# Splitting an expert's weights in quarter matrices on VectorE, between its tiles of h, instead of on GpSimd

## The reference, cut to what matters

```python
def _L0_ffn_ref(x, gate_weight, w1, b1, w2, b2):
    E, H = (8, 1024)
    logits = jnp.einsum('bld,ed->ble', x, gate_weight)
    kth_val = jnp.sort(logits.reshape(-1))[expert_k - 1]
    mask = (logits >= kth_val).astype(x.dtype)
    gates = logits * mask
    h = jax.nn.gelu(jnp.einsum('bld,ehd->bleh', x, w1) + b1, approximate=True)
    y = jnp.einsum('bleh,edh->blde', h, w2) + b2.T[None, None]
    return jnp.einsum('blde,ble->bld', y, gates)
x = x + jnp.tanh(g_xattn[0]) * _L0_xattn_ref(_layernorm(x), ctx_768, ...)
x = x + jnp.tanh(g_ffn[0]) * _L0_ffn_ref(_layernorm(x), ...)
```

## Time and profile before

| | |
|---|---|
| median of 3 runs | 2202.37 us (2200.15 to 2203.65) |
| the profiled execution: its time | 2204.5 us |
| its span | 2202.7 us |
| TensorE busy in the span | 2003.1 us (91%) |
| VectorE busy | 1359.9 us (62%) |
| ScalarE busy | 719.7 us (33%) |
| GpSimd busy | 230.9 us (10%) |
| granted clock of TensorE, mean | 0.958 |

### The profile page before, as it was taken

One profiled execution on the slowest core, in us unless ns is written; L12 is line 12 of the kernel. 1 busy time (PEld: TensorE's weight loads), 2 busy tenths in 40 slices (PEclk: granted clock), 3 DMA queues, 4 the chain that ended last, 5 costly groups with the idle time before them and its releaser, 6 DMA issues.

```text
span 2202.7 us, 29673 instructions
## 1 busy us (share of the span) xinstructions
PE 2003.1 (91%) x9252; PEld 1446.8 (66%) x9252; DVE 1359.9 (62%) x2389; ACT 719.7 (33%) x1206; POOL 230.9 (10%) x227
## 2 busy tenths in 40 slices
PE   3758999999975999899999989999998998999998
PEld 3643333333334788788778878877887886888887
DVE  7748888888836675645555465465456456454554
ACT  2224766666751222222222222222221222222222
POOL 5210111001114000200110020020002002000000
PEclk9877999999986999999999999999999999999999
DMA  3753322222201000100100010010001001000010
GB/s 108 242 190 111 81 77 73 71 79 78 62 30 60 0 28 18 48 10 15 38 20 14 10 48 14 10 48 14 10 13 49 10 10 47 14 10 15 29 43 34
DMA packets 80059, 103.39 MB, mean 47 GB/s; under 512 B 25986, under 2 KB 44164, under 8 KB 80004
## 3 DMA queue, kind: packets, MB, share of 16 engines
q1 hardware_dynamic: 80004, 102.71, 15.6%
HBM read 76.34 MB, written 26.08 MB: 46 GB/s over the span
## 4 chain that ended last, share of the span: by engine, by line
PE 63%; DVE 6%; ACT 0%; issue 0%; DVEq 0%; ACTq 0%
PE ps_y L1840 31%; PE ps_h L1826 31%; DVE h_lo L2047 3%; DVE h_hi L2043 2%; DVE candidate L2086 0%; ACT gelu L1946 0%; DVE w_hi L1986 0%; DVE gated L2112 0%; DVE out_T_acc L2117 0%; DVE w_lo L1988 0%; PE ps_h L1876 0%; DVE gate L2076 0%; DVE gate L2058 0%; PE ps_h L1908 0%; DVEq L1995 0%
## 5 line engine op out<-in xcount | busy, mean ns | idle before, releaser
L1946 ACT ACTIVATE gelu<-ps_h,b 128x512 f32<-128x512 f32 x512 | 352.0, 688 | 1153.6 <-PE ps_h L1826 1047.2
L2043 DVE CAST h_hi<-gelu 128x512 fp32r<-128x512 f32 x512 | 254.3, 497 | 601.5 <-ACT gelu L1946 601.2
L1840 PE MATMUL ps_y<-h_hi,w_hi 128*128 128x512 f32 x1024 | 410.3, 401 | 42.6 <-DVE h_lo L2047 42.6
L1826 PE MATMUL ps_h<-x_hi,w_hi 128*128 (+1 forms) x1024 | 413.5, 404 | 9.2 <-DVE w_lo L1988 9.2
L2047 DVE TENSOR_TENSOR h_lo<-gelu,h_hi 128x512 fp32r<-128x512 f32 x512 | 408.0, 797 | 16.5
L1826 PE MATMUL ps_h<-x_lo,w_hi 128*128 (+1 forms) x1024 | 411.0, 401 | 0.0
L1826 PE MATMUL ps_h<-x_hi,w_lo 128*128 (+1 forms) x1024 | 410.3, 401 | 0.0
L1840 PE MATMUL ps_y<-h_hi,w_lo 128*128 128x512 f32 x1024 | 408.0, 398 | 0.0
L1840 PE MATMUL ps_y<-h_lo,w_hi 128*128 128x512 f32 x1024 | 407.8, 398 | 0.0
L898 DVE TENSOR_REDUCE low<-ps_s 128x1 f32<-128x512 f32 x512 | 322.0, 683 | 39.8 <-PE ps_s L755 37.8
L1840 PEld LDWEIGHTS ps_y<-h_hi,w_hi 128*128 128x128 f32 x1024 | 195.3, 191 | 96.2 <-DVE h_lo L2047 48.3
(11 more groups left out here) (209 smaller groups left out, 1406.7 us busy)
## 6 DMA issues: line engine op xcount, KB each, us to landing
gate<-gates_scratch SPq DMA_DIRECT2D x64, 256.0 KB, 3.3
q_st<-q_scratch SPq DMA_DIRECT2D x64, 132.0 KB
k_scratch<-k_hl SPq DMA_DIRECT2D x32, 256.0 KB
q_scratch<-q_hl SPq DMA_DIRECT2D x32, 256.0 KB
k_st<-k_scratch SPq DMA_DIRECT2D x64, 128.0 KB
w_raw<-in_w1T SPq DMA_DIRECT2D x8, 1024.0 KB, 4.9
w_raw<-in_w2T SPq DMA_DIRECT2D x7, 1024.0 KB, 5.2
v_scratch<-v_out SPq DMA_DIRECT2D x8, 544.0 KB
```

What stands on the lines that cost most here:

```text
L1826: mm = pe.matmul(ps_h[:, j % RING, :], w[:, k, at], x[:, k, bass.ds(c * SEQ, SEQ)], start=(i == 0), stop=(i == len(parts) - 1))
L1840: mm = pe.matmul(ps_y[s][:, d, :], w[:, j, at], h[:, j % RING, :], start=(j == 0 and i == 0), stop=(j == HT - 1 and i == 2))
L1946: act.activation(gelu[:, j % GELUS, :], ps_h[:, j % RING, :], ACT.Gelu_apprx_tanh, bias=b1[p][:, j:j + 1]).then_inc(gelu_done, 1)
L2043: dve.tensor_copy(h_hi[:, j % RING, :], gelu[:, j % GELUS, :]).then_inc(h_hi_done, 1)
```

## The change

From the second expert on GpSimd no longer splits weights. VectorE does it, in pieces of a quarter matrix (128x512 elements): one instruction for `hi` behind one tile's `halves`, one for `lo` behind the next tile's. `PIECES_AT` gives the places (chunk, tile): w1 of the next expert is split behind tiles (1, 0), (1, 1), (1, 4) to (1, 7), (2, 0) and (2, 1), w2 behind (2, 6), (2, 7), (3, 0), (3, 1) and (3, 4) to (3, 7). Expert 1's weights are split during expert 0, four chunks later: in chunks 5 to 7 instead of during the search. The four first chunks of an expert are written out for VectorE, where two were. SyncE loads expert 1's w2 just before the gates of chunk 7.

```diff
+UNROLLED = 4
+PIECES = 4
+PIECES_AT = (((1, 0), (1, 1), (1, 4), (1, 5), (1, 6), (1, 7), (2, 0), (2, 1)),
+             ((2, 6), (2, 7), (3, 0), (3, 1), (3, 4), (3, 5), (3, 6), (3, 7)))
...
-            for half in range(2):
-                load_w(1, half)
+            load_w(1, 0)
...
             for i, c in enumerate(first_order):
+                if i == BATCH - 1:
+                    load_w(1, 1)
                 load_gate(0, c, c % 2, order=i)
...
-            def split(e, p, half, skip=0):
-
-                at = e * 2 + half
-                pool.wait_ge(raw_loaded[half], e * 16 + 16)
...
+            def split(half, skip):
+
+                pool.wait_ge(raw_loaded[half], 16)
+                hi, lo, raw = weight_views(0, half, first_w2 if half == 1 else w_raw, slice(skip, HT))
                 pool.tensor_tensor(hi, raw, zero[:].to_broadcast(hi.shape), ALU.add).then_inc(w_hi_done, 1)
-                pool.wait_ge(w_hi_done, at + 1)
+                pool.wait_ge(w_hi_done, half + 1)
                 pool.tensor_tensor(lo, raw, hi.bitcast(F32), ALU.subtract).then_inc(w_ready, 1)
 
             for half in range(2):
-                split(0, 0, half, skip=2 * LEAD if half == 0 else LEAD)
-            for half in range(2):
-                split(1, 1, half)
-            with pool.Fori(1, PAIRS) as pair:
-                for p in range(2):
-                    for half in range(2):
-                        split(pair * 2 + p, p, half)
+                split(half, 2 * LEAD if half == 0 else LEAD)
...
-            def chunk(e, c, before, tiles=range(HT)):
+            def chunk(e, c, before, tiles=range(HT), after=None):
                 for j in tiles:
                     halves(e, c, j)
                     if j == LEAD and before:
                         before()
-
-            def expert(e, p):
+                    if after:
+                        after(j)
+
+            def weight_piece(e, p, c, j):
+
+                for half, places in enumerate(PIECES_AT):
+                    if (c, j) not in places:
+                        continue
+                    i, part = divmod(places.index((c, j)), 2)
+                    done = ((e - 1) * 2 + half) * PIECES + i
+                    hi, lo, raw = weight_views(p, half, w_raw, slice(i * HT // PIECES, (i + 1) * HT // PIECES))
+                    if part == 0:
+                        if i == 0:
+                            dve.wait_ge(raw_loaded[half], e * 16 + 16)
+                        if i == 0 and half == 0:
+                            dve.wait_ge(w2_done, tile_no(e - 1, 0, 0) + RING)
+                        dve.tensor_copy(hi, raw).then_inc(w_hi_done, 1)
+                    else:
+                        dve.wait_ge(w_hi_done, 2 + done + 1)
+                        ins = dve.tensor_tensor(lo, raw, hi.bitcast(F32), ALU.subtract)
+                        if i == PIECES - 1:
+                            ins.then_inc(w_ready, 1)
+
+            def expert(e, p, last=False):
                 chunk(e, 0, lambda: add_chunk(e - 1, 1 - p, BATCH - 1, 1))
-                chunk(e, 1, lambda: add_chunk(e, p, 0, 0))
-                with dve.Fori(1, BATCH // 2) as cc:
+                for c in range(1, UNROLLED):
+                    chunk(e, c, lambda: add_chunk(e, p, c - 1, (c - 1) % 2),
+                          after=None if last else lambda j: weight_piece(e + 1, 1 - p, c, j))
+                with dve.Fori(UNROLLED // 2, BATCH // 2) as cc:
...
+            weight_piece(1, 1, 1, 0)
+            for c in range(SEARCH + 1, BATCH):
+                chunk(0, c, lambda: add_chunk(0, 0, c - 1, (c - 1) % 2), range(1 if c == SEARCH + 1 else 0, HT),
+                      lambda j: weight_piece(1, 1, c - SEARCH, j))
```

More of the change, by code:

```diff
@@ L2152, in _ @@
                     add_chunk(0, 0, c, c % 2, order=i)
-            chunk(0, SEARCH + 1, lambda: add_chunk(0, 0, SEARCH, 0), range(1, HT))
-            for c in range(SEARCH + 2, BATCH):
-                chunk(0, c, lambda: add_chunk(0, 0, c - 1, (c - 1) % 2))
+            weight_piece(1, 1, 1, 0)
+            for c in range(SEARCH + 1, BATCH):
+                chunk(0, c, lambda: add_chunk(0, 0, c - 1, (c - 1) % 2), range(1 if c == SEARCH + 1 else 0, HT),
+                      lambda j: weight_piece(1, 1, c - SEARCH, j))
             with dve.Fori(0, PAIRS - 1) as pair:
@@ L2158, in _ @@
                     expert(pair * 2 + i + 1, 1 - i)
-            expert(EXPERTS - 1, 1)
+            expert(EXPERTS - 1, 1, last=True)
             add_chunk(EXPERTS - 1, 1, BATCH - 1, 1)
```

## The result

The changed kernel takes 2128.64 us, the median of 4 runs (2127.29 to 2131.74), against 2203.01 us for the kernel before in the same comparison. The ratio is 0.9663, with a 95% interval of 0.9644 to 0.9682.

A forecast was written before the change was run, and what follows sets the result against it. TensorE's matmuls were taken to set the time in the experts' stage, with VectorE held up by GpSimd's splits. Terms -56.5 - 14.2 + 0.2 + 1.4 = -69.1 us took the 2202.37 us median to 2133.3, range 2129.5 to 2138.

The forecast's parts named there:

- The splits of experts 2 to 7: Experts' stage: with these 24 instructions off GpSimd, VectorE is no longer held up and tiles go at 2.80 us; -56.5 us.
- The search: Expert 0, tiles (0, 0, 4) to (0, 0, 7): expert 1's split leaves GpSimd there, 25.82 us becomes 11.6; -14.2 us.
- The pieces: VectorE in experts 1 to 6: one short piece fits into each tile's 1.64 us of idle time; term 0.
- dearer pieces: Rival: VectorE's pieces cost their long values, 2.117 + 2.743 us, losing 16 us in all, 2149 us; chance 0.04.
- After the additions: Expert 0, chunk 5: the first `hi` piece pushes `h_hi` back, TensorE waits; +0.2 us, between 0 and 0.5.
- The end of expert 0: Expert 1's last `lo` piece, behind (0, 7, 7), delays TensorE's first matmul of expert 1; +1.4 us once, bounds 0 to 3.5.
- The loads and the queue: VectorE's waits for weight loads have 7 and 8 us to spare, and SyncE's reordered gates come in time; both terms 0.
- Code fetched at jumps: Rival: VectorE's two jumps back each miss and cost TensorE 1.8 us, 2136.9 us; chance 0.04.
- The stall is not GpSimd's: Rival: VectorE's stall comes from the 1 MB loads, which stay, so nothing changes, 2202 us; chance 0.01.
- VectorE stuck behind a load: Rival: the wait for w2 behind (2, 6) holds every tile; a 27.5 us load gives 2207 us, slower; chance 0.01.

The follow-up runs named there:

- again: The kernel before and the changed kernel, each run again with no edit: 2200.53 us and 2129.26 us.
- start: Kernel before and changed kernel, each with GpSimd's first-stage fills waiting for VectorE's first four xn operations: 2197.83 us and 2131.55 us.
- spaced: Kernel before and changed kernel, each with GpSimd's first-stage fills issued one at a time, each waiting for the one before: 2197.16 us and 2126.12 us.
- whole matrices: The changed kernel with VectorE splitting whole matrices (128x2048) instead of quarters: 2137.39 us, 0.9689 of before.
- gpsimd_idle_adds: The changed kernel with GpSimd doing additions and subtractions of the old splits' size on an unused buffer in experts 1 to 6: 2163.69 us.
- quarters: The kernel before with GpSimd still splitting, but in quarter matrices from expert 1 on: 2135.96 us, 0.9681 of before.

## Why the prediction was wrong

The step that failed is the last one, from the sum to the time. It put the difference of all that lies ahead of tile (0, 0, 4) at nothing, and left room only for the spread of the runs shown, 3.5 us. What the runs showed in its place: that tile comes 6.80 us earlier in the profile of after. Over the 14 profiles the last stage starts anywhere from 663.6 to 678.1 us. Of this about 7 us are the first stage's draw (31.6 or 24.4 us to the first matmul), and the second stage takes 503.9 to 512.5 us. The profile of before that the sum was made against had the longer draw; that of after had the shorter.

Each kernel and its counterpart (before and after, again, start, spaced) give one pair of profiles. Behind tile (0, 0, 4) the change wins 68.9, 69.2, 69.8 and 72.4 us in them, 70.1 on average. Ahead of it the difference is 6.8, 5.7, -6.0 and 5.2 us. So the 69.1 of the sum is right for what it adds up, about 1 us low, and the part that it left out is as large as its error. The measured step of 74.4 us has an interval of 70.1 to 78.4, by that of the ratio. It is a step between medians, mostly of executions without a profile, so how its last 4 us are made up is not shown. That the medians of the spaced pair came out 71.0 us apart, near the sum, is in part luck: its two profiles are 77.6 us apart.

- *The splits of experts 2 to 7* (-56.5): right in cause and in this pair of profiles (-56.47). As an average it was a little too small. The other three profiles of the old splits lose 57.3, 57.7 and 59.7 us, so one execution was taken for all; the four average 57.8.
- *The search* (-14.2): right, 14.20. Expert 1 put back on GpSimd brings 14.45 back.
- *The pieces* (0): right, 0.42 and 0.69 us, and no tile late. The rival of dearer pieces falls. But the reason, that one short piece fits into the idle time of a tile, was given too narrowly: even whole matrices, whose `lo` is longer than the idle time, cost experts 1 to 6 nothing.
- *After the additions* (+0.2): 0.24. *The end of expert 0* (+1.4): 1.49. Both go away with the pieces moved.
- *The loads and the queue* (0): right. No piece of VectorE waited for a load in after.
- *Code fetched at jumps*: no row of after shows such a wait in the experts' stage; six experts are 0.01 us from the undisturbed time.
- *The stall is not GpSimd's*: refuted by gpsimd_idle_adds, which has a stall with no transfer beside it, and by after, which has the transfers without the stall.
- *VectorE stuck behind a load*: did not happen, with w2's pieces two tiles earlier neither; with whole matrices one piece waited 1.49 us in expert 0. (By its own terms this rival comes to 2208 us at a load of 27.5 us, 10.7 x 7 more than the forecast, and not to 2207.)

What stays open: why the second stage differs by up to 8.6 us between profiles, whether the first stage's draw falls with the execution or with the build, and why the runs of the kernel before spread over more (2194.01 to 2214.69 in 23 of them) than those of after (2125.83 to 2133.22 in 9). A part of the latter may be the stalls themselves: the six experts lose 56.5 to 59.7 us over four profiles of the old splits and 0.0 in each of the new.

## What to carry to other kernels

When two engines hold each other up, first look how long one operation holds and whether the waiting engine has a lead; cutting the long operations in quarters, on the engine where they were, was worth 67.4 of the 68.9 us in the last stage. A run of operations on GpSimd without a wait between them can hold a small operation of VectorE for the whole run, so keep it away from a start-up chain, or try a wait between its operations: here, with waits, the four xn operations took 6.43 us in three profiles out of three instead of 9.54 or 16.73. And before a sum from one profile is given a narrow range, ask what the untouched stages do from one execution to the next: here they differed by up to 6.8 us in a pair of profiles, more than the forecast's error of 4.7.

## What the runs showed of the hardware

- VectorE can get its turn between two GpSimd operations, where GpSimd waits on itself between them and also where it does not (quarters: `h_hi` 1.24 us and `h_lo` 1.66 beside operations of 1.04 to 1.49, `h_lo` before a `hi` that no wait holds back). In a run of fills that follow each other at once it is sometimes passed over to the end (7.95 us for an operation of 4 elements per partition, and 0.75 for the same one in another profile; 16.73 for four of 256). With waits between the fills this was not seen in three profiles. What decides it is not shown.
- GpSimd pays for the turns as well: the same split of 128x512 takes 1.04 us when it comes first and 1.49 where VectorE has its turn before it.
- A GpSimd fill holds VectorE's copy (up to 1.86 us) and leaves its subtraction of two SBUF operands alone (0.695 at most).
